# A vision tower on one core: the first attention's output projection goes from float32 to float32r on split operands, with the low half made on VectorE

## What is computed

```
q = einsum('bsd,hde->bshe', x, W_Q) + b_Q      # 12 heads of 64
k = einsum('bsd,hde->bshe', x, W_K) + b_K
v = einsum('bsd,hde->bshe', x, W_V) + b_V
scores = einsum('bqhe,bkhe->bhqk', q, k) / sqrt(64), causal mask
z = einsum('bhqk,bkhe->bqhe', softmax(scores), v)
h = layernorm(h + einsum('bqhe,hed->bqd', z, W_O) + b_O)
```

## Time and profile before

| | |
|---|---|
| median of three runs | 899.01 us |
| the profiled execution | 903.05 us |
| its span, first to last instruction | 901.3 us |
| first attention, within the span | about 62 to 291 us |
| TensorE busy over the span | 818.9 us, 91% |
| VectorE busy | 542.0 us, 60% |
| ScalarE busy | 439.9 us, 49% |
| GpSimd busy | 408.7 us, 45% |
| mean granted TensorE clock | 0.961 of full speed |

### The profile page before, as it was taken

The page is one execution under the profiler, slowest core; times in us unless marked ns, Lnnn a source line. Parts: engine busy times, 40 slices in busy tenths (PEclk is TensorE's granted clock), DMA queues, the critical chain, the costliest instruction groups (busy, mean ns, idle before and its releaser), DMA issues. The chain is left out here.

```text
span 901.3 us, 21350 instructions
## 1 busy us (share of the span) xinstructions
PE 818.9 (91%) x7767; PEld 733.5 (81%) x7767; DVE 542.0 (60%) x1467; ACT 439.9 (49%) x1094; POOL 408.7 (45%) x489
## 2 busy tenths in 40 slices
PE   9899999999998898987999989888879999999973
PEld 8889998899997676766999976666657899899973
DVE  2235565556665898993763337788966622467645
ACT  0246555555644576763345527566626221355523
POOL 1534444344444544342442236767841455244444
PEclk9999999999999999996999989898979999999996
DMA  9910111111110232225200013623200111333252
GB/s 308 265 51 21 31 27 37 31 32 30 37 37 2 35 67 26 34 22 172 24 1 1 1 27 50 157 47 65 46 3 2 36 60 63 81 99 107 77 170 94
DMA packets 103942, 55.78 MB, mean 62 GB/s; under 512 B 67264, under 2 KB 94512, under 8 KB 103840
## 3 DMA queue, kind: packets, MB, share of 16 engines
q1 hardware_dynamic: 99248, 45.99, 21.2%
q0 software_dynamic: 3792, 7.84, 2.5%
q10 hardware_dynamic: 800, 0.59, 0.2%
HBM read 29.81 MB, written 13.97 MB: 49 GB/s over the span
## 5 line engine op out<-in xcount | busy, mean ns | idle before, releaser
L931 POOL TENSOR_TENSOR attn_prob<-attn_prob,attn_recip 100x432 f32<-100x432 f32 x64 | 58.6, 916 | 67.1 <-DVE attn_recip L1316 66.6
L450 POOL TENSOR_TENSOR attn_prob_x<-attn_prob,attn_recip 100x864 f32<-100x864 f32 x32 | 52.6, 1644 | 52.8 <-DVE attn_recip L759 52.8
L1892 POOL DMA_INDIRECT results<-moe_hid_shared x43 | 41.1, 955 | 58.1 <-ACT moe_hid_shared L2107 58.1
L1602 ACT ACTIVATE mlp_hid<-psum,columns 128x384 f32<-128x384 f32 x72 | 38.1, 580 | 41.4 <-PE psum L96 41.4
L1047 PE MATMUL psum<-ident,attn_prob 100*108 100x100 f32 x256 | 35.5, 264 | 21.4 <-POOL attn_prob L931 12.9
L1047 PEld LDWEIGHTS psum<-ident,attn_prob 100*108 100x108 f32 x256 | 26.1, 138 | 27.2 <-POOL attn_prob L931 18.7
L1064 PEld LDWEIGHTS psum<-attn_prob_t,attn_values 108*49 108x49 f32 (+1 forms) x1024 | 33.7, 132 | 15.5 <-ACT attn_prob_t L1183 6.7
L1176 ACT ACTIVATE attn_prob<-attn_prob 100x432 f32<-100x432 f32 x64 | 36.1, 564 | 19.0 <-POOL attn_prob L938 17.8
L2082 ACT ACTIVATE moe_silu<-psum 128x384 f32<-128x384 f32 x36 | 17.7, 491 | 56.5 <-PE psum L107 56.5
L1064 PE MATMUL psum<-attn_prob_t,attn_values 108*49 108x36 f32 (+1 forms) x1024 | 36.0, 217 | 8.3 <-DMA attn_values<-attn_v_tok 5.0
L1555 PE MATMUL psum<-mlp_w_dn_s,mlp_hid 128*128 128x192 f32 (+2 forms) x306 | 42.6, 290 | 0.0
(11 more groups left out here) (474 smaller groups left out, 2790.5 us busy)
## 6 DMA issues: line engine op xcount, KB each, us to landing
embed_patches<-in_x SPq DMA_DIRECT2D x8, 768.0 KB, 14.5
sorted_rows<-mlp_pad_zeros SPq DMA_DIRECT2D x1, 4214.0 KB, 15.6
moe_hid_shared<-sorted_rows SPq DMA_DIRECT2D x43, 98.0 KB, 2.1
attn_v<-attn_v_tok SPq DMA_DIRECT2D x16, 216.0 KB
attn_values<-attn_v_tok SPq DMA_DIRECT2D x96, 27.0 KB
side_raw_a<-in_w_gu_dram SPq DMA_DIRECT2D x8, 288.0 KB, 3.2
side_raw_b<-in_w_gu_dram SPq DMA_DIRECT2D x16, 144.0 KB, 3.4
h_rows<-results SPq DMA_DIRECT2D x6, 288.0 KB, 5.4
```

The source lines that it names most:

```text
L450: nc.gpsimd.tensor_tensor(prob_x[k % 2][:, :, :, :], prob[k % 3][:, :, :].rearrange("p h (a n) -> p h a n", a=1) .to_broadcast([QP, HEADS, ...
L931: nc.gpsimd.tensor_tensor(pr, pr, recip[k % 2][:, :].rearrange("p (h a) -> p h a", a=1) .to_broadcast([QP, HEADS, SEQ]), ALU.mult).then_in ...
L1602: nc.scalar.activation(hid_step(n), bank(n % 3)[:, 0:MW], ACT.Gelu, bias=b_up[:, c:c + 1]).then_inc(S["gelu_done"], 1)
L1892: nc.gpsimd.indirect_dma_start(out=results, out_offset=bass.IndirectOffsetOnAxis(ap=x_in[j % x_ring][:, D:D + 1].bitcast(U32), axis=0), in ...
```

## The change

The mixed heads are kept as a high part `z_hi`, which ScalarE writes by a copy that rounds to float32r, and a low part `z_lo`, which VectorE makes as z minus `z_hi`, reading z from PSUM bank 6 once more (`split_z`). `w_o` is split in the same way, once: `w_o_hi` on ScalarE ahead of the first step, `w_o_lo` on VectorE in step 1. Each chunk of `project_out` is now three float32r matmuls. What waited for ScalarE's copy (`z_copied`) now waits for VectorE's subtraction (`low_made`, which also counts the split of the weights, hence the 1 +): the next mix, the output projection, and `odd_banks_free`. The ring holds 2 tiles instead of 3; where a unit wraps around its end, copy and subtraction are two instructions each (`z_pieces`).

```diff
-    v_ring, vt_ring, z_ring = 5, 3, 3 * P
+    v_ring, vt_ring, z_ring = 5, 3, 2 * P
...
-        z_t = sb("z_t", [P, chunks, z_ring])
+        z_hi, z_lo = (sb(nm, [P, chunks, z_ring], F32R) for nm in ("z_hi", "z_lo"))
+        w_o_hi, w_o_lo = w_o_split
...
+        def z_pieces(k):
+            at = (k * UNIT) % z_ring
+            n = min(UNIT, z_ring - at)
+            return [(slice(at, at + n), slice(0, n)), (slice(0, UNIT - n), slice(n, UNIT))][:1 if n == UNIT else 2]
...
             def mix(k):
                 pe.wait_ge(S[f"v_landed{k % v_ring}"], landed[k])
                 if k >= 1:
-                    pe.wait_ge(S["z_copied"], k)
+                    pe.wait_ge(S["low_made"], 1 + k)
...
             def project_out(t):
-                pe.wait_ge(S["z_copied"], -(-P * (t + 1) // UNIT))
+                pe.wait_ge(S["low_made"], 1 + -(-P * (t + 1) // UNIT))
...
                 for c in range(chunks):
-                    last = nc.tensor.matmul(out_ps, z_t[:, c, at:at + P], w_o[:, c, :],
-                                            start=(c == 0), stop=(c == chunks - 1))
+                    hi, lo = z_hi[:, c, at:at + P], z_lo[:, c, at:at + P]
+                    nc.tensor.matmul(out_ps, hi, w_o_hi[:, c, :], start=(c == 0), stop=False)
+                    nc.tensor.matmul(out_ps, hi, w_o_lo[:, c, :], start=False, stop=False)
+                    last = nc.tensor.matmul(out_ps, lo, w_o_hi[:, c, :], start=False, stop=(c == chunks - 1))
...
             def odd_banks_free(k):
 
                 if k >= 3:
-                    pe.wait_ge(S["z_copied"], k - 2)
+                    pe.wait_ge(S["low_made"], 1 + k - 2)
...
-                ins = nc.scalar.activation(z_t[:, :, at:at + n], z_ps[:, :, 0:n], ACT.Copy)
-                if n < UNIT:
-                    ins = nc.scalar.activation(z_t[:, :, 0:UNIT - n], z_ps[:, :, n:UNIT], ACT.Copy)
-                ins.then_inc(S["z_copied"], 1)
+                for to, of in z_pieces(k):
+                    ins = nc.scalar.activation(z_hi[:, :, to], z_ps[:, :, of], ACT.Copy)
+                ins.then_inc(S["high_made"], 1)
...
+            small["scalar"](act)
+            nc.scalar.activation(w_o_hi[:, :, :], w_o[:, :, :], ACT.Copy).then_inc(S["high_made"], 1)
...
+            def split_z(k):
+                dve.wait_ge(S["high_made"], 1 + k + 1)
+                for to, of in z_pieces(k):
+                    ins = nc.vector.tensor_tensor(z_lo[:, :, to], z_ps[:, :, of], z_hi[:, :, to].bitcast(F32),
+                                                  ALU.subtract)
+                ins.then_inc(S["low_made"], 1)
...
                 if k < units:
                     take_scores(k)
+                if k == 1:
+                    dve.wait_ge(S["high_made"], 1)
+                    nc.vector.tensor_tensor(w_o_lo[:, :, :], w_o[:, :, :], w_o_hi[:, :, :].bitcast(F32), ALU.subtract
+                                            ).then_inc(S["low_made"], 1)
+                if k >= 3:
+                    split_z(k - 3)
                 if g < groups and j < 3:
                     copy_k_high(g, 2 * j)
```

More of the change, by code:

```diff
@@ L337, in keep_going, with wide_stage @@
         nc.tensor.matmul(out[:, 0:2 * D], ident[:, :], constants, start=True, stop=True)
-def wide_stage(nc, kept, small, psum, ident, neg_half, name, rings, make_following, h_tok, w_q, w_k, w_v, w_o, bias, q_bias, k_bias, out_bias):
+def wide_stage(nc, kept, small, psum, ident, neg_half, name, rings, make_following, h_tok, w_q, w_k, w_v, w_o, w_o_split, bias, q_bias, k_bias, out_bias):
     groups, units = TOK // WIDE, TOK // UNIT
@@ L683, in copy_z @@
                     act.wait_ge(S["out_done"], over // P + 1)
-                at = (k * UNIT) % z_ring
-                n = min(UNIT, z_ring - at)
-                ins = nc.scalar.activation(z_t[:, :, at:at + n], z_ps[:, :, 0:n], ACT.Copy)
-                if n < UNIT:
-                    ins = nc.scalar.activation(z_t[:, :, 0:UNIT - n], z_ps[:, :, n:UNIT], ACT.Copy)
-                ins.then_inc(S["z_copied"], 1)
+                for to, of in z_pieces(k):
+                    ins = nc.scalar.activation(z_hi[:, :, to], z_ps[:, :, of], ACT.Copy)
+                ins.then_inc(S["high_made"], 1)
             for c in range(chunks):
@@ L2673, in build @@
             w_o1 = fsb("w_o1", [P, 6, D])
+            w_o1_split = [fsb(n, [P, 6, D], F32R) for n in ("w_o1_hi", "w_o1_lo")]
             bias1 = fsb("bias1", [QP, SEQ])
@@ L2788, in sync, with scalar @@
                     sp.wait_ge(S["bias_row_placed"], 16)
+                def scalar(act):
+                    act.wait_ge(S["value_bias_done"], 1)
                 def out_bias_ready(pool):
                     pool.wait_ge(S["out_biases_ready"], 1)
-                later.update({"sync": sync, "tensor": tensor, "vector": vector, "gpsimd": out_bias_ready})
+                later.update({"sync": sync, "tensor": tensor, "scalar": scalar, "vector": vector, "gpsimd": out_bias_ready})
                 return {"load": load, "load_columns": load_columns, "scale_columns": scale_columns,
@@ L2809, in first_of_attn2 @@
                 return FirstTokens(nc, psum, ident, neg_half, h_tok, rings, (0, 1), ("y_ready", 3), norm_cols(0), room)
-            wide_stage(nc, kept, later, psum, ident, neg_half, "attn1", rings, first_of_attn2, h_tok, w_q1, w_k1, w_v1, w_o1, bias1, q_bias1,
+            wide_stage(nc, kept, later, psum, ident, neg_half, "attn1", rings, first_of_attn2, h_tok, w_q1, w_k1, w_v1, w_o1, w_o1_split, bias1, q_bias1,
                        k_bias1, out_bias1)
```

## The result

The changed kernel takes 937.95 us (median of 4 runs, 930.91 to 941.2), against 899.96 us for the kernel before in 4 runs beside it: a ratio of 1.0415 (95% interval 1.0343 to 1.0487). Forecast were 932.5 us and 914 to 946. The profiled execution took 941.2 us, with a span of 939.5 us; it is the longest of the four.

A forecast was written before the change was run, and what follows sets the result against it. The prediction took TensorE to bound the stage, busy 220.8 of 228.0 us. Its terms, 23.4 (new wait) + 8.1 (last steps) + 2.0 (projection) = 33.5 us on 899.0, gave 932.5 us, range 914 to 946.

The forecast's parts named there:

- The new wait: In 18 loop steps the odd q chunk waits for VectorE's subtraction to free bank 6: 23.4 us.
- the gaps of 8.3 us: Over those 18 steps, how far VectorE's maximum ends behind the odd chunk's start before the change: in sum 8.3 us.
- It feeds on itself: In the loop, when TensorE slips VectorE slips with it, so the next step stalls anew and the stall stays.
- The rival by which only half of them would stall: In the loop only about every second step stalls, and the tail by half: 917 us or less, 9%.
- The last seven steps: Output projection and mix wait for the subtraction at the first attention's end: 8.1 us, or 4 if partly absorbed.
- The chain of delays: Delays growing through the last steps: +3.1 us in step 29, +5.8 in 31, +7.4 in 33, +8.1 at the last projection.
- the row of the second attention: Profile row cited for a clock fall: after a gap of 1.24 us the granted clock was 0.52 over 3.5 us.
- the fourth rival: TensorE's clock falls behind the waits in half of the 18 loop steps: 15 us more, 948 us, 10%.
- TensorE's own work: Output projection, 18 float32r records a tile for 12, paced by loads at 0.111 us each: +2.0 us.
- the upper bound of this term: Output projection records at 0.131 us apiece: +0.49 us a tile, +8.8 us in all.
- The edits costed at nothing: Splitting w_o, ScalarE's extra copy pieces and the shorter ring are covered: no cost, 1 us together if a cover is gone.
- its 1.6 for the projection: The loop's part, for 14 tiles, of the forecast cost of the float32r output projection: 1.6 us.

The follow-up runs named there:

- e1: Changed kernel with the output projection back in float32, subtraction and all its waits kept: 936.27 us, ratio 1.0424 to the kernel before.
- e2: Changed kernel with VectorE's subtraction moved ahead of take_scores, right behind sum_up: 909.05 us, ratio 1.0122 to the kernel before.
- e5: Changed kernel with four float32 filler matmuls ahead of the output projection in steps 29 and 31: 932.55 us, ratio 1.0361 to the kernel before.
- e4: Changed kernel with the output projection streaming only 96 of its 192 columns, half the result left out: 941.87 us, one run.
- e6: e2 with the low part of w_o split in step 0 instead of step 1: 909.89 us, ratio 1.0130 to the kernel before.
- e3: Changed kernel where a second, full ScalarE copy frees bank 6 and VectorE subtracts from SBUF: 928.53 us, ratio 1.0340 to the kernel before.
- e8: e7 with k before q in odd chunks, subtraction ahead of row sums from step 32, fillers in steps 29 and 31: 905.53 us, ratio 1.0050.
- e9: e8 with the last four tiles projected in float32 without subtraction, fillers and other tail edit removed: 897.93 us, ratio 0.9989 to the kernel before.
- e7: e6 with high and low w_o side by side, 12 records a tile for 18, VectorE adding both halves: 910.50 us, ratio 1.0137.

## Why the prediction was right, and where its sizes were off

**The new wait, right.** 18 waits in the steps named, caused by the place of the subtraction in VectorE's order: e1 has all of the loss without the float32r records, e2 has little of it with them. The term was 23.4 us, and it measured 21.0 in e1 (196.42 less 175.41): the gaps of 8.3 us stand, but the odd chunk starts 0.57 us after the maximum's end (0.64 with two pieces, in 6 of the 18 steps) and not 0.69 and 0.84. 8.3 + 12 x 0.57 + 6 x 0.64 + 18 x 0.10 = 20.8, and with the projection's 0.6 it makes 21.4 of the measured 21.6. I had set 0.03 us between VectorE's instructions, where the subtraction's row overlaps the maximum's by 0.08, and 0.15 for a second piece, which costs 0.07 (two pieces in 0.66 us).

**It feeds on itself, right.** VectorE slipped with TensorE, and all 18 steps stall. The rival by which only half of them would stall is refuted by the count.

**The last seven steps, the mis-sized term: 16.0 us for 8.1.** The chain of delays was right link by link, as e5 shows. What failed is the clock: I looked for the fall in the loop, whose waits are about 1 us, and not behind the waits that I had myself put at 3 us in the last steps. There the row of the second attention applied, and 20.5 us ran at the lower level up to 319 us, 23.9 in all. e5, which fills two of the waits, takes 5.4 us off the last steps. So the fourth rival happened, in another place and, by e5, at a third of its 15 us. What the falls cost in the runs that were not profiled is not known: the profiled one is the longest of the four, with a mean clock of 0.953, and the shortest (930.91 us) has 0.962.

**TensorE's own work, right in kind, small in size.** 0.112 us a record was forecast as 0.111, and e4 shows that the stream doesn't pace it. The term was +2.0 us, and the loop shows +0.6 for 14 tiles. A tile's busy time grew by 0.09 us (2.23 for 2.14), near the forecast 0.11, but its first record comes 0.06 us sooner behind the matmul ahead, so that only 0.03 to 0.04 us a tile are lost; that the busy time is not the whole distance I left out. (In the upper bound of this term, 0.131 us a record gives by the same sum about 0.46 us a tile and 8.2 us, not 0.49 and 8.8.) The Trainium skill's figures (TensorE: Matmul & The Clock Gate, section on the back-to-back issue gap) would have given 89 ns, an estimate between its figures. The measurement's 112 ns is nearer to the 107 ns for 128 columns by the same page's section on loading the stationary operand.

**The edits costed at nothing.** The low part of `w_o` was put at 1.4 us and harmless. It took 2.62 us, and the head grew by 1.34. In e6, where it starts ahead of GpSimd, it takes 1.35 us, as forecast; what I left out is that GpSimd works beside it. The traces show the two engines in each other's way where VectorE reads two operands from SBUF (e6, e3), and not where it reads one from PSUM (600 ns beside GpSimd's 913). The Trainium skill (SBUF — State Buffer, section Who interferes with whom) states that a VectorE instruction with two inputs in SBUF contends with a GpSimd instruction that reads SBUF, and one with at most one such input, outside some modes, does not. These rows agree.

**Sum.** 21.6 + 16.0 + 1.3 + 0.3 - 1.1 = 38.2 us between the profiled spans, against 33.5; 38.0 between the medians. The loop was overrated by 3.4 us (its 1.6 for the projection included) and the last steps underrated by 7.5. That the two errors partly cancel is luck, and part of why the time came out 5.5 us from the forecast.

**What stays open.** What each of the two edits in e8's tail gave, which were not made apart. How much of the median, and not of the profiled execution, the falls of the clock cost. Nor was it tried whether e9's loop can be shortened further by taking the second add off VectorE.

## What to carry to other kernels

Before a piece of work is given to an engine that looks half idle, read the timeline for the moment at which it is free and the moment at which its result is wanted: the same 0.6 us instruction in every step, with what came of it, cost 38 us or 11, by its place among three others. If a change adds waits of different lengths, look for a fall of the clock behind the longest first, at the ends of pipelines, where nothing else covers them. And count loads: here three float32r matmuls for one float32 matmul (18 records a tile for 12) cost 0.03 us a tile, and gained 0.23 only when two of them shared a stationary operand in one record.

## What the runs showed of the hardware

- Records with 128 stationary columns in float32r start 0.112 us apart with 192 and with 96 moving columns at the full clock (changed kernel, e4), and 0.21 us apart at the lower level. A pair of 384 and 192 columns takes 0.29 us (e7).
- A VectorE subtraction with both operands in SBUF took 1055 ns in the mean (e3) where the one with an operand in PSUM took 508 (changed kernel), and GpSimd's subtraction of the same stage went from 913 to 1136 ns. Single rows look as if they took turns: 1.35 us for VectorE and 1.96 instead of 0.91 for GpSimd in e6, 2.62 for VectorE in the changed kernel.
- 18 waits of 0.7 to 1.3 us, in steps of some 8 us, left the clock at its upper level for 200 us (changed kernel). In waits of 2.8 and 2.9 us it fell, for 6.8 and 13.7 us. The length of one wait does not decide alone: in the last steps of e8 the clock fell for 3.4 us behind a wait of 1.4 us, with waits of 1.1 and 1.2 us ahead of it.
